# Softmax of the messages: one exponent per slot on ScalarE behind two VectorE instructions, and the message one-hots all on ScalarE

## What is computed

```python
en = feat_src[src]; ev = feat_dst[dst]
e = jnp.sum(leaky_relu(en + ev) * attn, axis=-1, keepdims=True)
m = segment_max(e, dst); ee = jnp.exp(e - m[dst])
alpha = ee / jnp.maximum(segment_sum(ee, dst)[dst], 1e-9)
msg = jax.nn.softmax(en * r_feat * alpha, axis=-1)      # over 32 features, per edge and head
g_sum = jnp.sum(segment_sum(msg, dst), axis=1)
```

## Time and profile before

| | before |
|---|---|
| median of 3 runs | 4073.04 us (4067.71 to 4081.34) |
| the profiled execution's own time | 4068.59 us |
| its span | 4066.6 us |
| PE, busy | 3054.0 us (75%) |
| VectorE (DVE), busy | 2564.1 us (63%) |
| ScalarE (ACT), busy | 2697.1 us (66%) |
| GpSimd (POOL), busy | 2903.5 us (71%) |
| gathers of the third pass (L1945) | 1,564 instructions, the first starts at 1870.0 us, the last at 3897.6 us |

### The profile page before, as it was taken

One profiled execution on the slowest core, in us unless ns is written; L12 is line 12 of the kernel. 1 busy time (PEld: TensorE's weight loads), 2 busy tenths in 40 slices (PEclk: granted clock), 3 DMA queues, 4 the chain that ended last, 5 costly groups with the idle time before them and its releaser, 6 DMA issues. The chain is left out here.

```text
span 4066.6 us, 79597 instructions
## 1 busy us (share of the span) xinstructions
PE 3054.0 (75%) x26497; PEld 2336.8 (57%) x26497; DVE 2564.1 (63%) x7531; ACT 2697.1 (66%) x7419; POOL 2903.5 (71%) x2913
## 2 busy tenths in 40 slices
PE   4899999999798998885566666766766667666655
PEld 2555555666466666665465555665656666556544
DVE  7987766555422222235357777778777787777776
ACT  4888888778665556641056767777668766677745
POOL 4677777776377777755777777777777777777735
PEclk9999999999899999997657777777667776677767
DMA  2455565555588888853333333333333433343311
GB/s 79 186 207 207 211 234 208 206 207 206 195 310 279 291 289 284 284 173 107 64 86 85 83 81 87 89 86 84 79 82 93 91 83 83 77 92 87 87 31 41
DMA packets 294489, 592.92 MB, mean 146 GB/s; under 512 B 121210, under 2 KB 205364, under 8 KB 286169
## 3 DMA queue, kind: packets, MB, share of 16 engines
q1 hardware_dynamic: 203920, 515.15, 36.0%
q0 software_dynamic: 88192, 72.56, 11.0%
q10 hardware_dynamic: 1969, 0.10, 0.0%
HBM read 384.60 MB, written 202.94 MB: 144 GB/s over the span
## 5 line engine op out<-in xcount | busy, mean ns | idle before, releaser
L897 ACT ACTIVATE scratch<-sum_x_ps_c 128x600 bf16<-128x600 f32 (+7 forms) x1003 | 775.4, 826 | 168.1 <-PE sum_x_ps_c L934 156.5
L1945 POOL DMA_INDIRECT scratch<-fs_scratch,src_idx x728 | 725.3, 996 | 221.9 <-issue 221.9
L834 POOL DMA_INDIRECT gath<-in_x,src_idx x620 | 673.2, 1086 | 277.4 <-issue 182.4
L834 POOL DMA_INDIRECT gath<-y_scratch,src_idx x540 | 524.2, 971 | 171.6 <-issue 163.4
L2073 ACT ACTIVATE scratch<-scratch,bias,weight 128x32 f32<-128x32 f32 x1360 | 484.0, 399 | 101.5 <-DVE bias L2143 101.5
L1987 PEld LDWEIGHTS ps_e<-fdw,scratch 128*128 128x128 f32 x3136 | 500.4, 242 | 24.2
L934 PE MATMUL sum_x_ps_c<-e_tab,scratch 128*128 128x300 bf16 (+7 forms) x2006 | 472.9, 323 | 51.9 <-DVE scratch L1012 32.3
L1009 DVE TENSOR_SCALAR e_tab<-scratch 128x1300 bf16<-128x1300 f16 (+13 forms) x1024 | 455.7, 458 | 61.0 <-PE sum_x_ps_c L934 53.0
L1987 PE MATMUL ps_e<-fdw,scratch 128*128 128x66 f32 x3136 | 482.7, 322 | 0.0
L2154 DVE SCALAR_TENSOR_TENSOR scratch<-ps_e,attn_sb 128x128 f32<-128x128 f32 x784 | 190.2, 285 | 424.3 <-PE ps_e L1987 423.3
L963 PEld LDWEIGHTS sum_x_ps_d<-parts,scratch 128*128 128x128 bf16 x5800 | 337.1, 98 | 158.7 <-ACT scratch L897 68.0
(11 more groups left out here) (341 smaller groups left out, 6362.9 us busy)
## 6 DMA issues: line engine op xcount, KB each, us to landing
count_scratch<-scratch SPq DMA_DIRECT2D x58, 3200.0 KB
scratch<-count_scratch SPq DMA_DIRECT2D x232, 800.0 KB
onehot<-rel_scratch SPq DMA_DIRECT2D x196, 256.0 KB
scratch<-in_edge_attr_2x SPq DMA_DIRECT2D x390, 128.0 KB
fdw<-fd_scratch SPq DMA_DIRECT2D x392, 33.0 KB
scratch<-fs_scratch,src_idx POOLq DMA_INDIRECT x728
gath<-in_x,src_idx POOLq DMA_INDIRECT x652
gath<-y_scratch,src_idx POOLq DMA_INDIRECT x540
```

The costliest lines, as they stand in the source:

```text
L834: pool.indirect_dma_start(out=gath[:, s, t, 0:F], out_offset=None, in_=table_dram, in_offset=bass.IndirectOffsetOnAxis(ap=src_idx[:, g, k: ...
L897: act.activation(to, ps_c[u % pairs][:, :, 0:q].rearrange("p h (d a) -> p h a d", d=d), ACT.Copy).then_inc(kept, 1)
L1945: pool.indirect_dma_start(out=rows_of(m)[:, t, :], out_offset=None, in_=fs_dram, in_offset=bass.IndirectOffsetOnAxis(ap=src_idx[:, g, k:k ...
```

## The change

The walk's sixteen exponents per slot become the form that the tail had: VectorE subtracts the maximum from all 512 values of a partition and then multiplies them by a, each as one instruction with an operand that is repeated over 32 features (`each`), and ScalarE computes one exponent of 128x512. With that, VectorE's sum covers all eight edges of a partition and not the last four. The tables `weight` and the instructions L2140 and L2143 go. `onehot_on_vector` no longer names the even slots, so ScalarE makes these 89 one-hots too. Four slots late in the tail keep theirs on VectorE.

```diff
             def onehot_on_vector(n):
 
-                return on_vector(n, 0) or (0 < n <= TAIL and n % 2 == 0)
+                return on_vector(n, 0)
...
                         if m is None:
 
                             act.wait_ge(scaled, n - (TAIL - 1))
-                            act.activation(rows_of(n)[:, :, 0:HID], rows_of(n)[:, :, 0:HID], ACT.Exp).then_inc(exp_done, 1)
                         else:
-                            act.wait_ge(bias_ready, n + 1)
-                        for i in range(ST * H if m is not None else 0):
-                            rows = rows_of(n)[:, i // H, i % H * F:(i % H + 1) * F]
-                            e = act.activation(rows, rows, ACT.Exp, bias=bias[:, q, i:i + 1],
-                                               scale=weight[:, q, i:i + 1],
-                                               accum_out=total[:, q, i:i + 1] if i < K * H else None)
-                        if m is not None:
-                            e.then_inc(exp_done, 1)
+                            act.wait_ge(weighted, n + 1)
+                        act.activation(rows_of(n)[:, :, 0:HID], rows_of(n)[:, :, 0:HID], ACT.Exp).then_inc(exp_done, 1)
...
                     if exists(n, 0) and m is not None:
-                        dve.tensor_copy(weight[:, q, :],
-                                        attention_of(n))
+                        heads = rows_of(n)[:, :, 0:HID].rearrange("p t (h f) -> p t h f", h=H)
                         dve.wait_ge(top_ready, n + 1)
-                        dve.scalar_tensor_tensor(bias[:, q, :], top[:, :], -1.0,
-                                                 attention_of(n),
-                                                 ALU.mult, ALU.mult).then_inc(bias_ready, 1)
+                        dve.tensor_tensor(heads, heads, each(top[:, :]), ALU.subtract).then_inc(lowered, 1)
+                        dve.wait_ge(lowered, n + 1)
+                        dve.tensor_tensor(heads, heads, each(attention_of(n)), ALU.mult).then_inc(weighted, 1)
...
-                        first = K if m is not None else 0
                         dve.wait_ge(exp_done, n)
-                        dve.tensor_reduce(total[:, q1, first * H:], rows_of(n - 1)[:, first:, 0:HID]
+                        dve.tensor_reduce(total[:, q1, :], rows_of(n - 1)[:, :, 0:HID]
```

More of the change, by code:

```diff
@@ L1736, in build @@
             top = sb("top", [P, ST * H], F32, ctx)
-            weight = sb("weight", [P, SLOTS, ST * H], F32, ctx)
             bias = sb("bias", [P, SLOTS, ST * H], F32, ctx)
@@ L1769, in build @@
             loaded = [sem(f"loaded{s}") for s in range(SLOTS)]
-            (multiplied, top_ready, bias_ready, exp_done, sum_ready, rec_ready, msg_ready, oh_msg_ready, summed,
-             added) = map(sem, ("multiplied", "top_ready", "bias_ready", "exp_done", "sum_ready", "rec_ready",
+            (multiplied, top_ready, lowered, weighted, exp_done, sum_ready, rec_ready, msg_ready, oh_msg_ready, summed,
+             added) = map(sem, ("multiplied", "top_ready", "lowered", "weighted", "exp_done", "sum_ready", "rec_ready",
                                 "msg_ready", "oh_msg_ready", "summed", "added"))
@@ L1828, in rows_of, with each @@
                 return kept_spare[:, q, :, :] if q < IN_SPARE else kept_nodes[:, q - IN_SPARE, :, :]
+            def each(columns):
+                return wide(columns.rearrange("p (t h) -> p t h", h=H), 3, [P, ST, H, F])
             def attention_of(n):
@@ L1951, in heads @@
                     return rows_of(n)[:, :, 0:HID].rearrange("p t (h f) -> p t h f", h=H)
-                def each(columns):
-                    return wide(columns.rearrange("p (t h) -> p t h", h=H), 3, [P, ST, H, F])
                 def step(m, n, q, piece):
```

## The result

| | before | after |
|---|---|---|
| median of the runs | 4072.63 us (4067.61 to 4081.34, 5 runs) | 4091.3 us (4089.04 to 4093.27, 5 runs) |
| span of the profiled execution | 4066.6 us | 4090.8 us |
| gathers of the third pass, busy | 1552.2 us | 1566.4 us |
| VectorE, busy | 2564.1 us | 2705.8 us |
| ScalarE, busy | 2697.1 us | 2110.7 us |

The ratio is 1.0052, with a 95% interval of 1.0039 to 1.0066: the change makes the kernel slower by 0.5%, some 21 us. The forecast was no change, 4068 us within 4048 to 4094. The time lies inside the range, near its upper end, but the change left the 0.3% in which I had put it.

A forecast was written before the change was run, and what follows sets the result against it. GpSimd's unpaused gather issue was taken to bound the third pass, with VectorE instructions holding gathers up. From 4068.6 us, -23.8 + 20.0 - 0.8 gave 4064.0 us in the profile, 4068 us as a median, range 4048 to 4094.

The forecast's parts named there:

- What bounds the kernel: Third pass: GpSimd issues gathers without pause; VectorE instructions with two SBUF inputs lengthen them, 75.8 us above the median's total.
- The one-hots go, -23.8 us: Third pass: 87 VectorE one-hots before the last gather move to ScalarE, so gathers lose 23.8 us less.
- The pair comes, +20.0 us: Third pass: 358 new 128x512 VectorE instructions hold gathers up by 0.056 us each, L2129's price, +20.0 us.
- The end of the walk, -0.8 us: From step 192 on VectorE runs late; fewer one-hots against the pair and wider sum give -0.8 us.
- ScalarE, and VectorE's work, at nothing: Per slot ScalarE falls from 7.4 to 4.1 us, VectorE rises from 7.8 to 8.6; neither changes the time.
- Rival 2: Third pass: every pair meets a gather start, 0.24 us a pair, 43 us in all; median 4091 us, slower; chance 0.17.
- Rival 1: Third pass: the pair hardly meets a gather, 0.02 us per instruction, 7 us in all; median 4055 us, faster; chance 0.27.
- Rival 3: Third pass: VectorE becomes the bound, needing 0.65 us more per step than counted; chance 0.03.

The follow-up runs named there:

- one-hots alone: The kernel before, with all message one-hots on ScalarE and its 16 exponents per slot kept; 4062.73 us, 0.9982 of before.
- the reduction: The kernel before with message one-hots on ScalarE and an unread reduction over 1,024 values in each old one-hot's place on VectorE; 4066.14 us, 0.9978 of before.
- the pair in PSUM: The changed kernel, with the small operand of both new instructions (the maxima, a copy of the 16 values a) in PSUM; 4064.3 us, 0.9986 of before.
- the reciprocals in PSUM: The kernel before with message one-hots on ScalarE and the reciprocals that L2196 scales with written to PSUM; 4059.75 us, 0.9964 of before.
- L2129 in four: The kernel before with message one-hots on ScalarE, L2196's reciprocals in PSUM and L2129 split into four instructions; 4071.32 us, 0.9994 of before.

## Why the prediction was wrong

By its steps:

- **What bounds the kernel**: right. The gathers' issue sets the pass, their excess is what is left of a VectorE instruction at their start less 0.13 us, and reductions and instructions with a PSUM input do not hold them. All twelve profiles agree, and an edit that moved two small operands to PSUM took 23 us off the gathers.
- **The one-hots go, -23.8 us**: this is the step that failed. The runs showed -7.3 us without the pair and -3.2 with it. The 23.8 us were truly lost behind the one-hots, but they were not theirs to give back: a held gather and its successors are put in step with VectorE, and L2196 and L2129 right behind passed between two starts because of it. Without the hold they met more of them: L2129 went from 36 late gathers and 9.8 us to 88 and 25.1 without the pair, and to 103 and 22.8 in the change itself. I had used this very fact, 1.12 us from a hold's end to the next start, to argue for a cheap pair, and did not apply it to what I took out.
- **The pair comes, +20.0 us**: right in size, 18.5 and 22.6 us by the two comparisons. The gathers late behind the pair itself lost 27.9 us; some of that came off other lines. By the row that I chose, L2129's 0.056 us, it was right partly by chance, since that low price was itself made by the one-hots.
- **The end of the walk, -0.8 us**: not to be told. From the last gather to the end it is 168.1 and 169.7 us before, 171.6 and 168.2 after.
- **ScalarE, and VectorE's work, at nothing**: right. Nothing waited for an exponent more than before, and VectorE with 1244 us of 1398 still kept up.
- **Rival 2**, each pair meets a gather: its mechanism is what happened, 177 of 177, at 0.16 us a pair and not 0.24. With the one-hots' 23.8 us and the 27.9 measured, its sum would have given 4072 us in the profile and no slowdown. Its time, 4091, is the measured one only because two errors cancel. Rival 1 (the pair hardly meets one) is out, though 62 pairs went by its very steps (a gather held by the scaling, the next late in the target one-hot, the third near the end of the subtraction); it did not have the 103 gathers that L2121 held, whose second successor falls into L2136. Rival 3 is out too: GpSimd never waited for a release longer than its own gap.

The sum with what was measured: 4067.6 (mean span before) - 7.3 + 22.6 + 4.7 (start and end, within an execution's variation) = 4087.6, the mean span after.

What was not tried: a kernel in which L2129, too, has a PSUM operand. Its second operand is 512 columns wide, and none of the block's eight PSUM tiles has that much free.

## What to carry to other kernels

When one engine's issue is the pace and another engine's instructions hold it up, ask of every instruction on that other engine whether its operands come from SBUF or from PSUM, and price the whole chain between two pauses, not each instruction: taking one holder out of a chain mostly hands its cost to the next. A small operand (a maximum, a reciprocal, a column) that is kept in a spare corner of a PSUM tile took the hold away here: at the same duration for the pair and for L2196, and for 0.46 us more where it displaced a faster instruction, L2097. Work taken off an engine for which nobody waits, like ScalarE's 445 us in the steady stretch, is worth nothing, while what replaces it may hold up the engine that sets the pace.

## What the runs showed of the hardware that I had not expected

- By the Trainium skill, "SBUF — State Buffer", section "Who interferes with whom", the inference from a probe was that a `tensor_tensor` does not stall the descriptors of a GpSimd DMA. For these indirect gathers it does, to the end of the instruction: 177 gathers of 177 that started inside the pair were late, and 0 of 177 once one operand was in PSUM. The measurement decides.
- Four `tensor_tensor` of 128x128 with no wait between them hold a gather that starts in the second or third to the end of the fourth (82 of 82; 1.42 us in the one shown), but one that starts in the first only to the end of that one (10 of 10).
- The gathers' excess was 66 to 68 us in five kernels with very different sets of holders (one-hots alone, the reduction, the pair in PSUM, the reciprocals in PSUM, L2129 in four), and fell to 49 and 45 us only when the last chain longer than the 1.25 us between two gather starts was broken.
